# Two neighbouring matmuls of 128 columns as one of 256, with the sum of the two parts moved to VectorE, in two gathers of a graph network

## What is computed

```python
def gcn_conv(x, w, b, src, dst, deg_inv_sqrt):
    h = x @ w
    norm = deg_inv_sqrt[src] * deg_inv_sqrt[dst]
    msg = h[src] * norm[:, None]
    out = jax.ops.segment_sum(msg, dst, num_segments=N)
    return out + b
...
h = batchnorm(x, g_in, be_in)
h = jax.nn.relu(batchnorm(gcn_conv(h, w1, b1, src, dst, deg_inv_sqrt), g1, be1))
h = jax.nn.relu(batchnorm(gcn_conv(h, w2, b2, src, dst, deg_inv_sqrt), g2, be2))
```

## Time and profile before

| | us |
|---|---|
| median of 3 runs | 2834.3 (2833.37 to 2838.01) |
| the profiled execution | 2861.55 |
| its span, first to last instruction | 2859.7 |
| first gather, first matmul to last drain | 1279.54 to 1357.60 |
| second gather, the same | 1418.33 to 1496.93 |

### The profile page before, as it was taken

How to read it: one execution, slowest core, us unless ns; L and a number is a source line. 1 busy time by engine, 2 the same in 40 slices (tenths; PEclk the granted TensorE clock), 3 DMA queues, 4 the chain that set the end, 5 groups by cost and what they waited for, 6 DMA issues and landing times. The chain is left out here.

```text
span 2859.7 us, 90081 instructions
## 1 busy us (share of the span) xinstructions
PE 2092.1 (73%) x33857; PEld 1846.2 (65%) x33857; DVE 2223.9 (78%) x4347; ACT 1831.8 (64%) x3004; POOL 158.2 (6%) x143
## 2 busy tenths in 40 slices
PE   0069978949959959939593998768995898766644
PEld 0045544638949949839482898768994898656622
DVE  2999978958878878761517999889997999849953
ACT  0059977957757666520205999599996999535421
POOL 0331133100000000000000000000000000000000
PEclk9979999979979979969796999889997999878867
DMA  2224534544314324227262333043312333034100
GB/s 80 87 86 189 229 158 163 225 159 125 123 63 142 106 90 147 73 65 226 77 210 77 107 102 91 17 127 95 108 56 81 104 101 97 8 105 128 57 8 23
DMA packets 186835, 308.74 MB, mean 108 GB/s; under 512 B 6718, under 2 KB 163265, under 8 KB 186446
## 3 DMA queue, kind: packets, MB, share of 16 engines
q1 hardware_dynamic: 185626, 303.77, 32.1%
q0 software_dynamic: 960, 1.26, 0.2%
HBM read 220.45 MB, written 88.67 MB: 108 GB/s over the span
## 5 line engine op out<-in xcount | busy, mean ns | idle before, releaser
L372 ACT ACTIVATE stage<-ps 125x375 f32 x625 | 314.0, 604 | 150.5 <-PE ps L317 146.1
L270 DVE TENSOR_SCALAR col<-iota_col,window_col 125x376 bf16<-125x376 f16 x1250 | 334.4, 336 | 33.4 <-PE ps L317 33.4
L317 PE MATMUL ps<-col,lo 125*125 125x375 bf16 x1250 | 288.1, 346 | 41.9 <-DVE col L270 41.7
L936 ACT ACTIVATE r2amsk<-r2ad,r2thr 125x640 f16 x360 | 259.9, 815 | 0.4 <-DVE r2asel L958 0.3
L936 ACT ACTIVATE r0amsk<-r0ad,r0thr 125x640 f16 x360 | 259.6, 814 | 0.1
L936 ACT ACTIVATE r1amsk<-r1ad,r1thr 125x640 f16 x360 | 259.6, 815 | 0.1
L1009 PE MATMUL ps<-r2mv,r2asel 125*128 125x66 f16 x5000 | 244.1, 196 | 6.6 <-issue 5.4
L317 PEld LDWEIGHTS ps<-col,lo 125*125 125x125 bf16 x1250 | 140.8, 141 | 163.0 <-DVE col L270 157.5
L1009 PE MATMUL ps<-r1mv,r1asel 125*128 125x66 f16 x5000 | 243.3, 196 | 2.7 <-issue 1.6
L1009 PE MATMUL ps<-r0mv,r0asel 125*128 125x66 f16 x5000 | 243.1, 196 | 1.3 <-DVE r0asel L958 0.5
L1009 PEld LDWEIGHTS ps<-r2mv,r2asel 125*128 125x128 f16 x5000 | 227.4, 100 | 10.4 <-issue 5.9
(11 more groups left out here) (532 smaller groups left out, 4480.8 us busy)
## 6 DMA issues: line engine op xcount, KB each, us to landing
counts<-stage SPq DMA_DIRECT2D x75, 800.0 KB, 4.8
ct<-counts_all SPq DMA_DIRECT2D x75, 800.0 KB, 4.6
counts_all<-total SPq DMA_DIRECT2D x25, 800.0 KB, 7.3
g0ct<-counts_all SPq DMA_DIRECT2D x25, 800.0 KB, 4.5
g1ct<-counts_all SPq DMA_DIRECT2D x25, 800.0 KB, 4.5
g2ct<-counts_all SPq DMA_DIRECT2D x25, 800.0 KB, 4.6
r0ct<-counts SPq DMA_DIRECT2D x25, 800.0 KB, 5.1
r1ct<-counts SPq DMA_DIRECT2D x25, 800.0 KB, 4.7
```

What stands on the lines that cost most here:

```text
L270: ins = v.tensor_scalar(col1[:, b % OHS * WIN + w], K.iota_col[:], K.window_col[:, bass.ds(i * (P // DG) + b, 1), w], None, ALU.is_equal)
L317: ins = pe.matmul(K.ps[0:P, s, 0:GW], lo1[:, b, 0:P, w], col1[:, s * WIN + w, 0:GW], start=(w == 0), stop=(w == WIN - 1))
L372: act.activation(dst.rearrange("p a r h d -> p (a r h) d"), K.ps[0:P, b % OHS, 0:GW].rearrange("p (x d) -> p x d", d=DG), ACT.Copy).then_i ...
L936: act.activation(msk[:, s % 5, n], ad[:, bass.ds(g % 2, 1), h] .rearrange("p a (b d) -> p (a b) d", d=PAD), ACT.Sigmoid, bias=T.thr[:, 1, ...
```

## The change

Each pair of matmuls becomes one, of 256 columns: `parts[:, s]` with both parts in a row is the moving operand, and the result goes to 256 columns of the bank, high and low apart. It has one weight load in place of two. DVE drains 256 columns in one instruction into a new SBUF buffer `both`, and after the fifth drain adds the two halves of each block into `z`, in five more instructions. A new semaphore `added` counts them, and DVE waits for it at the end of a round.

```diff
-    used, full, drained = S(tag + "_used"), S(tag + "_full"), S(tag + "_drained")
-    with nc.Block() as block:
+    used, full, drained, added = (S(tag + "_" + n) for n in ("used", "full", "drained", "added"))
+    with nc.Block() as block, nc.sbuf_tensor(tag + "sum", [P, 5, 2, D], F32) as both:
...
-                        for p in range(2):
-                            ins = pe.matmul(K.ps[:, b, 0:D], ct[0:P, s // 5, b, s % 5], parts[:, s, p],
-                                            start=(s == 0 and p == 0), stop=(s == NB - 1 and p == 1))
+                        ins = pe.matmul(K.ps[:, b, 0:2 * D], ct[0:P, s // 5, b, s % 5],
+                                        parts[:, s].rearrange("p a f -> p (a f)"),
+                                        start=(s == 0), stop=(s == NB - 1))
...
-                    v.tensor_scalar(dst[:, bass.ds(5 * g + b, 1)].rearrange("p a f -> p (a f)"), K.ps[0:P, b, 0:D],
+                    v.tensor_scalar(both[:, b].rearrange("p a f -> p (a f)"), K.ps[0:P, b, 0:2 * D],
                                     K.dinv[:, bass.ds(5 * g + b, 1)], span, ALU.mult, ALU.mult).then_inc(drained, 1)
+                for b in range(5):
+                    v.wait_ge(drained, 5 * g + b + 6)
+                    v.tensor_tensor(dst[:, bass.ds(5 * g + b, 1)].rearrange("p a f -> p (a f)"), both[:, b, 0],
+                                    both[:, b, 1], ALU.add).then_inc(added, 1)
+                v.wait_ge(added, 5 * g + 5)
```

## The result

| | before | changed |
|---|---|---|
| median of 11 runs, us | 2834.3 (2827.8 to 2838.2) | 2844.1 (2840.1 to 2848.0) |
| ratio, 95% interval | | 1.0034 (1.0025 to 1.0044) |
| profiled execution / its span, us | 2861.55 / 2859.7 | 2845.23 / 2843.4 |

The forecast was 2842.9 us, +8.6; measured is +9.8. In a second set, of 10 runs, the changed kernel had a ratio of 1.0040 (1.0012 to 1.0067).

What follows compares the result with a forecast made beforehand. PE was taken to bound the rounds, waiting for DVE at each border. Terms -3.0 + 5.5 + 4.1 + 2.0 = +8.6 us on the median 2834.3 gave 2842.9 us, 0.3% slower; range 2837.5 to 2849.0.

Steps and rivals of the forecast that it cites:

- The stream: Matmuls inside the rounds: each merged pair gains only 0.0024 us, -3.0 us for both gathers (0 to -3.8).
- A border: Between rounds of a gather: longer drains lengthen PE's wait by 0.69 us per border, +5.5 us for both gathers.
- The rival with fixed drains: Borders and gather ends: drain time is fixed, extra columns ride along; +1.5 us in all, 2836, no change; chance 0.07.
- The end of a gather: After the last round: later and longer drains, uncovered adds and a wait, 2.03 us each, +4.1 us for both.
- The clock behind the gathers: Stages behind each gather: longer PE idling lowers the clock, 1.6 us behind the first, 0.4 behind the second, +2.0 us.
- (1): Behind the gathers: the clock holds despite the longer gap; +6.6 us or a little less, 2839 to 2841; chance 0.16.
- (2): The rival with fixed drains, by its number: +1.5 us, 2836; chance 0.07.
- (3): Inside the gathers: the longer stall at the borders drops the clock; +7 us on top, 2850; chance 0.09.
- (4): In the stream: a pair costs only its one weight load, 0.100 us; sum -2.5 us, 2832; chance 0.04.
- (5): Elsewhere: something else, such as DMA loads, moves as much; left as no change; chance 0.04.

Runs made afterwards that it cites:

- e1: Kernel before with the merged 256-column matmuls, but the old 128-column drain and no adds (low parts left out of the sum); ratio 0.9993 against before.
- e3: Changed kernel plus 30 filler matmuls of zeros behind PE's last round of each gather; ratio 1.0007 against before, 0.9982 in the second set.
- e4: Kernel before with the gather's blocks placed in eight PSUM banks in turn instead of five, rounds unrolled; ratio 0.9962 against before.

## Where the prediction held, and where it did not

**The stream** held: a step of 0.109 in the changed kernel, e1 alone -1.44 and -1.06 for the gathers, -1.5 and a little back predicted. The Trainium skill, "TensorE: Matmul & The Clock Gate", section "Back-to-back issue gap", would give 98 ns as an estimate on its line for pairs of weight load and matmul. This trace does not agree: it has 109.

**A border** held: rounds of 15.50 (15.5 predicted), drains of 0.535 and a step of 0.45. The rival with fixed drains had the earlier trace rows for it, another instruction with another fixed part; the slope of L545 was the better guide, since it is the same kind of instruction.

**The end of a gather** was a little too dear: the five adds take 1.09, not 1.13 and their start, and PE's gap is 3.57 where 3.7 was predicted. In the first gather all three terms together are +2.9, 3.3 predicted.

**The clock behind the gathers** held: it fell, and the first transposes cost 1.5 more (1.6 predicted), the second 0.14 (0.4 predicted). e3 took just these back. The reason that I gave for it, the length of the gap, is not the whole of it: 2.39 us did both.

**What was missing.** The four terms as measured are +2.9 and +1.9 for the gathers and +1.6 behind them, 6.4 in all, where 8.6 was forecast. Of the 2.2 us that are missing, 0.8 are the gathers' terms, 0.4 too dear in each; 0.4 are the transposes; and 1.0 is what the second gather gained because it met less of the low clock in its first round. The other 3.8 of the 10.2 us have no term at all. 1.2 lie between the gathers, where the 100 matmuls of L1404 (L1399 before) take 14.01 us at a mean clock of 0.79 and took 12.84 at 0.86. 2.6 are in "rest", nearly all of them in the attention stages. The change touches none of this code. The step in which the sum failed is that it ends with the transposes and puts everything behind them at nothing, without a reason; the sentence that nothing of the 27 us depends on the change, which is right, does not cover it. So the total was met (+8.6 against +9.8) more closely than its parts deserve: terms 2.2 us too dear and 3.8 us without a term nearly cancel, and that is luck.

The rivals: the clock did not hold (1), drains are not fixed (2), the clock did not fall at the borders (3; it is 1.00 from 1268.9 to 1330.6 and from 1412.8 to 1474.5, the last four rounds of each gather), pairs don't go under their columns (4), the loads stayed hidden (5; 0.85 of the DMA engines, 0.94 even in e4).

## What to carry to other kernels

Merging matmuls that share a weight block gains only the fixed bit of an instruction when the loads already run beside the columns; look at the step of the stream against its columns before counting loads. What PSUM accumulates on the way is dear to add up later: the second half of the columns has to be drained by DVE at the very places where PE waits for DVE, and at the end of a gather nothing covers the adds either. And where PE waits for drained banks, ask first for unused banks: three of them were worth 0.95 us at each border.

## What the hardware showed that I had not expected

A change of a few microseconds can move stages far behind it by 3 to 6 us each, up or down, for the same instructions (275.7 to 278.5 us in the first attention stage of e3, 281.9 before, 283.7 in the changed kernel), as far as the traces tell by where in the stage the clock is low. For two of the three kernels that were profiled twice it did so reproducibly, within 0.05 us over the 1350 us of "rest"; for the third, e3, the two executions are 3.4 us apart. So a second profile need not average it out. Three kernels that differ by 2.1, 4.2 and 7.0 us of plain delay took the same time in their profiles, though not in their medians. A difference below some 5 us in this kernel should be read stage by stage, from the profile, before it is put down to the edit. Also, the clock both held and fell across gaps of 2.39 us.
